# A graph network of four layers: the update pass reordered, the degree taken into the root, and eight row buffers in the heads pass

## The reference

```
x = layernorm(x + L0(x))   # two GAT convolutions, then concat(x, out2) @ Wu + bu
x = layernorm(x + L1(x))   # 12 heads of 64: relu(res + attention-weighted sum)
x = layernorm(x + L2(x))   # GCN: D^-1/2 A D^-1/2 (x W) + b
x = layernorm(x + L3(x))   # two GCN convolutions with a relu between
layernorm(x) = (x - mean) / sqrt(var + 1e-5)
```

## Time and profile before

| | us |
|---|---|
| median of 3 runs (lowest, highest) | 3884.01 (3877.66, 3886.38) |
| the profiled execution | 3883.69 |
| its span | 3881.9 |
| TensorE busy | 3556.3 (92%) |
| VectorE busy | 2481.6 (64%) |
| ScalarE busy | 1366.8 (35%) |
| GpSimd busy | 1092.4 (28%) |

### The profile page before, as it was taken

One profiled execution on the slowest core, in us unless ns is written; L12 is line 12 of the kernel. 1 busy time (PEld: TensorE's weight loads), 2 busy tenths in 40 slices (PEclk: granted clock), 3 DMA queues, 4 the chain that ended last, 5 costly groups with the idle time before them and its releaser, 6 DMA issues. The chain is left out here.

```text
span 3881.9 us, 64638 instructions
## 1 busy us (share of the span) xinstructions
PE 3556.3 (92%) x21125; PEld 3356.1 (86%) x21125; DVE 2481.6 (64%) x4955; ACT 1366.8 (35%) x1888; POOL 1092.4 (28%) x1533
## 2 busy tenths in 40 slices
PE   7999999999999888258996999998899998899999
PEld 6999999999999544138995999997899998799999
DVE  4877986158433588347996777776344443577777
ACT  2222232222222344115664344443333332344443
POOL 5540200414512100427774222221222221322221
PEclk9999999999999999679998999999999999999999
DMA  4777887658754688425665333334333333455554
GB/s 113 238 235 212 238 250 242 190 184 268 225 180 142 198 251 253 139 75 173 212 212 177 104 127 126 126 127 144 108 126 125 127 128 117 157 183 186 184 184 142
DMA packets 363376, 672.37 MB, mean 173 GB/s; under 512 B 100181, under 2 KB 193010, under 8 KB 363242
## 3 DMA queue, kind: packets, MB, share of 16 engines
q1 hardware_dynamic: 248154, 441.01, 37.3%
q10 hardware_dynamic: 70160, 155.79, 10.3%
q0 software_dynamic: 44928, 73.84, 6.8%
HBM read 429.79 MB, written 346.94 MB: 200 GB/s over the span
## 5 line engine op out<-in xcount | busy, mean ns | idle before, releaser
L716 DVE TENSOR_TENSOR fr_lo<-fr_turned_ps,fr_hi 128x768 fp32r<-128x768 f32 x158 | 150.4, 952 | 240.0 <-ACT fr_hi L1140 240.0
L1592 PE MATMUL up_prod<-w_up,up_ot 128*128 128x396 f32 x632 | 231.4, 510 | 40.9 <-DVE up_y L1496 40.9
L2408 DVE SCALAR_TENSOR_TENSOR c3a_y<-c3a_prod,dinv,next_const 128x768 f32<-128x768 f32 x79 | 80.4, 1018 | 288.8 <-PE c3a_prod L2564 288.8
L1284 PE MATMUL fr_prod<-fr_w_hi,fr_hi 128*128 128x396 f32 x948 | 257.1, 352 | 0.0
L1284 PE MATMUL fr_prod<-fr_wu_hi,fr_hi 128*128 128x396 f32 x948 | 254.7, 349 | 0.0
L1284 PE MATMUL fr_prod<-fr_w_lo,fr_hi 128*128 128x396 f32 x948 | 249.3, 344 | 0.0
L2564 PE MATMUL cv_prod<-next_w_hi,cv_hi 128*128 128x384 f32 x948 | 248.9, 344 | 0.0
L2564 PE MATMUL c3a_prod<-next_w_hi,c3a_hi 128*128 128x384 f32 x948 | 248.9, 344 | 0.0
L1284 PE MATMUL fr_prod<-fr_w_hi,fr_lo 128*128 128x396 f32 x948 | 248.7, 343 | 0.0
L2564 PE MATMUL c3b_prod<-next_w_hi,c3b_hi 128*128 128x384 f32 x948 | 248.6, 344 | 0.0
L1284 PE MATMUL fr_prod<-fr_wu_lo,fr_hi 128*128 128x396 f32 x948 | 248.3, 343 | 0.0
(11 more groups left out here) (588 smaller groups left out, 9109.0 us busy)
## 6 DMA issues: line engine op xcount, KB each, us to landing
fr_ins<-in_x_dram SPq DMA_DIRECT2D x156, 384.0 KB, 4.2
x<-fr_zrow SPq DMA_DIRECT2D x156, 384.0 KB
x<-up_x_o ACTq DMA_DIRECT2D x78, 396.5 KB, 3.5
h<-fr_outs SPq DMA_DIRECT2D x78, 396.0 KB
u<-fr_outs SPq DMA_DIRECT2D x78, 396.0 KB
up_ut<-u SPq DMA_DIRECT2D x78, 396.0 KB
agg<-fr_zrow SPq DMA_DIRECT2D x78, 390.0 KB
hds_row<-x SPq DMA_DIRECT2D x78, 384.0 KB, 3.2
```

The costliest lines, as they stand in the source:

```text
L716: v.tensor_tensor(lo[:, s2, :, :], turned_ps[:, 0:KC, :], hi[:, s2, :, :].bitcast(F32), ALU.subtract).then_inc(split_done, 1)
L1284: made = nc.tensor.matmul(prods[s2][:, bank, 0:c1 - c0], l[:, s2, s, :], w[:, s, c0:c1], start=(s == 0 and i == 0), stop=(s == KC - 1 and ...
L1592: made = nc.tensor.matmul(prods[s2][:, half, 0:HALFC], ot[:, s2, k, :], g["w_up"][:, k, half * HALFC:(half + 1) * HALFC], start=(k == 0), ...
L2408: v.scalar_tensor_tensor(y3, p3, g["dinv"][:, bass.ds(t, 1)], c3, ALU.mult, ALU.add).then_inc(prod_read, 1)
```

## The change

Update pass: y gets four buffers instead of two. VectorE's step does y and the statistics of tile t-2 first, and then the shift of tile t-3. The wait for the polish moves from before y to before the reciprocal, and asks for the tile before.

Heads pass and first convolution: 1 / sqrt(var + eps) times dinv is computed as 1 / sqrt(deg x var + deg x eps). The degree and its product with eps stand in two new columns, made in the first stage; ScalarE's root takes them as scale and bias, and VectorE's product with dinv goes.

Heads pass: eight buffers for the rows of x1, and the loop body of all engines there holds eight tiles; the other buffers stay four.

```
+            link(v.tensor_copy(g["deg"][:, :], pt["deg"][:, :]))
+            link(v.tensor_scalar(g["deg_eps"][:, :], pt["deg"][:, :], EPS, None, ALU.mult))
...
# update_pass
-        y = sb("y", [P, 2, CU])
+        y = sb("y", [P, UNROLL, CU])
...
                 dve.wait_ge(multiplied, t + 1)
-                if at_least(t, 2):
-                    dve.wait_ge(polished, t - 1)
-                v.tensor_tensor(y[:, s2, :].rearrange("p (a f) -> p a f", a=2), prods[s2][:, :, 0:HALFC],
+                v.tensor_tensor(y[:, slot, :].rearrange("p (a f) -> p a f", a=2), prods[s2][:, :, 0:HALFC],
...
             def shift_of(t, slot, turn):
                 s2 = slot % 2
                 dve.wait_ge(rooted, t + 1)
+                if at_least(t, 1):
+                    dve.wait_ge(polished, t)
                 v.reciprocal(rstd[:, s2, :], root[:, s2, :]).then_inc(shifted, 1)
...
             def step(t, slot, turn):
+                b = back(t, slot, turn, 2)
+                if at_least(t, 2) and live(b[0]):
+                    end(*b)
                 b = back(t, slot, turn, 3)
                 if at_least(t, 3) and live(b[0]):
                     shift_of(*b)
-                b = back(t, slot, turn, 2)
-                if at_least(t, 2) and live(b[0]):
-                    end(*b)
...
# heads_pass
-    H, F = 12, D
+    H, F, WIDE = 12, D, 2 * UNROLL
...
-        row, more = sb("row", [P, UNROLL, D]), sb("more", [P, UNROLL, AGG_W])
+        row, more = sb("row", [P, WIDE, D]), sb("more", [P, UNROLL, AGG_W])
...
-                if at_least(t, UNROLL):
-                    sp.wait_ge(prod_read, t - UNROLL + 1)
+                if at_least(t, WIDE):
+                    sp.wait_ge(prod_read, t - WIDE + 1)
                 sp.dma_start(row[0:rows_of(t), slot, :], tile_rows(x1, t)[:, 0:D]).then_inc(loaded[slot], 16)
-            over_tiles(sp, step)
+            over_tiles(sp, step, 0, WIDE)
...
                 v.reciprocal(rstd[:, s2, :], root[:, s2, :]).then_inc(shifted, 1)
-                dve.wait_ge(shifted, t * 3 + 1)
-                v.tensor_scalar(rstd[:, s2, :], rstd[:, s2, :], g["dinv"][:, bass.ds(t, 1)], None, ALU.mult).then_inc(shifted, 1)
-                dve.wait_ge(shifted, t * 3 + 2)
+                dve.wait_ge(shifted, t * 2 + 1)
...
-                nc.scalar.activation(root[:, slot % 2, :], mv[:, slot % 2, 1:2], ACT.Sqrt, bias=g["eps"][:, 0:1]).then_inc(rooted, 1)
+                nc.scalar.activation(root[:, slot % 2, :], mv[:, slot % 2, 1:2], ACT.Sqrt, bias=g["deg_eps"][:, bass.ds(t, 1)],
+                                     scale=g["deg"][:, bass.ds(t, 1)]).then_inc(rooted, 1)
```

More of the change, by code:

```diff
@@ L87, in at_least, with over_tiles, back @@
     return not isinstance(t, int) or t >= k
-def over_tiles(eng, step, drain=0):
-    for t in range(UNROLL):
+def over_tiles(eng, step, drain=0, unroll=UNROLL):
+    for t in range(unroll):
         step(t, t, 0)
[L95 to L104, removed]
+    with eng.Fori(1, NT // unroll) as i:
+        for j in range(unroll):
+            step(i * unroll + j, j, i)
+    for t in range(NT // unroll * unroll, NT + drain):
+        step(t, t % unroll, t // unroll)
+def back(t, slot, turn, lag, unroll=UNROLL):
+    return t - lag, (slot - lag) % unroll, turn + (slot - lag) // unroll
 def live(t):
@@ L1547, in polish @@
                     act.wait_ge(stored[slot], turn * 32)
-                nc.scalar.activation(x_o[:, slot, 0:D], y[:, s2, 0:D], ACT.Identity, bias=shift[:, s2, :],
+                nc.scalar.activation(x_o[:, slot, 0:D], y[:, slot, 0:D], ACT.Identity, bias=shift[:, s2, :],
                                      scale=rstd[:, s2, :]).then_inc(polished, 1)
@@ L2051, in heads_pass @@
         prods = [ctx.enter_context(nc.psum_tensor(f"hds_prod{i}", [P, 2, 512], F32)) for i in range(2)]
-        loaded = [sem(f"loaded{j}") for j in range(UNROLL)]
+        loaded = [sem(f"loaded{j}") for j in range(WIDE)]
         more_in = [sem(f"more_in{j}") for j in range(UNROLL)]
@@ L2102, in step @@
             def step(t, slot, turn):
-                b = back(t, slot, turn, -2)
+                b = back(t, slot, turn, -2, WIDE)
                 if live(b[0]):
                     fetch(*b)
-                b = back(t, slot, turn, -1)
+                b = back(t, slot, turn, -1, WIDE)
                 if live(b[0]):
@@ L2111, in _ @@
             scale(0, 0, 0)
-            over_tiles(pool, step)
+            over_tiles(pool, step, 0, WIDE)
         @block.vector
@@ L2167, in _ @@
             own(0, 0, 0)
-            over_tiles(dve, step, 3)
+            over_tiles(dve, step, 3, WIDE)
         @block.scalar
@@ L2238, in step @@
                     turn_over(t, slot, turn)
-                b = back(t, slot, turn, 1)
+                b = back(t, slot, turn, 1, WIDE)
                 if at_least(t, 1) and live(b[0]):
                     multiply(*b)
-            over_tiles(pe, step, 1)
+            over_tiles(pe, step, 1, WIDE)
 def conv_layer(nc, g, tag, table, out, weights, bias, res=None, first=False, last=False):
@@ L2256, in conv_layer @@
         L = 2 if apart else 1
-        K = 2 if last else 3
         rows_in = sb("row", [P, UNROLL, D])
@@ L2423, in shift_of @@
                 v.reciprocal(rstd[:, s2, :], root[:, s2, :]).then_inc(shifted, 1)
-                if not last:
-                    dve.wait_ge(shifted, t * K + 1)
-                    v.tensor_scalar(rstd[:, s2, :], rstd[:, s2, :], g["dinv"][:, bass.ds(t, 1)], None, ALU.mult).then_inc(shifted, 1)
-                dve.wait_ge(shifted, t * K + (K - 1))
+                dve.wait_ge(shifted, t * 2 + 1)
                 v.scalar_tensor_tensor(shift[:, s2, :], mv[:, s2, 0:1], -1.0, rstd[:, s2, :], ALU.mult, ALU.mult).then_inc(shifted, 1)
@@ L2478, in root_of @@
                 act.wait_ge(spread, t + 1)
-                nc.scalar.activation(root[:, slot % 2, :], mv[:, slot % 2, 1:2], ACT.Sqrt, bias=g["eps"][:, 0:1]).then_inc(rooted, 1)
+                if last:
+                    nc.scalar.activation(root[:, slot % 2, :], mv[:, slot % 2, 1:2], ACT.Sqrt, bias=g["eps"][:, 0:1]).then_inc(rooted, 1)
+                else:
+                    nc.scalar.activation(root[:, slot % 2, :], mv[:, slot % 2, 1:2], ACT.Sqrt, bias=g["deg_eps"][:, bass.ds(t, 1)],
+                                         scale=g["deg"][:, bass.ds(t, 1)]).then_inc(rooted, 1)
             def polish(t, slot, turn):
```

44 lines of the change are left out of this document (22 added, 22 removed).

## The result

| | before | after |
|---|---|---|
| median of 4 runs, us | 3881.35 (3877.66 to 3886.38) | 3821.43 (3819.79 to 3824.29) |
| profiled execution, us (span) | 3883.69 (3881.9) | 3824.29 (3822.6) |
| update pass, first to last y | 286.8, 3.677 a tile | 233.3, 2.991 a tile |
| heads pass, first to last y | 323.7, 4.150 a tile | 311.4, 3.992 a tile |
| the three convolutions, first to last y | 537.5, 537.6, 537.6 | 537.6, 537.6, 537.5 |

The ratio is 0.9846 (0.9829 to 0.9863): 60 us less, where I had forecast 3838 us, with 3826 as the best end of the range. In the spans the two passes give 53.5 + 12.3 = 65.8 us and the rest of the kernel takes 6.5 back.

What follows compares the result with a forecast made beforehand. Prediction: a VectorE wait chain bounds the update pass, TensorE nearly bounds the heads pass. 3883.7 less 35.6 (update) and 10.5 (heads) gave 3837.6, rounded to 3838 us; range 3826 to 3866 us.

Steps and rivals of the forecast that it cites:

- the DMA floor lies between 3.04 and 3.19 us: Update pass: least time a tile's 916 KB need, from 301 GB/s elsewhere and 287 GB/s at share 1.
- 3.22 us, a little above the highest: Update pass: tile period forecast just above the highest of three engine floors, saving 35.6 us.
- 3.64 - 0.36 - 0.20 = 3.08 us: Update pass: VectorE's period without the root and polish waits; 3.14 us on average with the loop turn's 3.31.
- Bounds: 3.12 us (43 us saved): Update pass: best case of the tile period; the worst was 3.5 us, 14 us saved.
- its floor is at most 3.12 us: Update pass: TensorE's time a tile, from its 0.52 us idle in each 3.64.
- hidden with about 1.1 us to spare: Update pass: the 1.01 us polish ends before VectorE's 2.3 us of y and statistics, so the moved wait costs nothing.
- TensorE's 3.99 us is the floor: Heads pass: TensorE limits each tile to 3.99 us, 311.2 us in all, 12.5 us below the pass then.
- The longer loop and the earlier rows: Heads pass: fewer loop turns bring VectorE's period to 3.68 us; earlier row loads end GpSimd's 25.6 us of waits.
- slack to catch up: Heads pass: VectorE gets 0.3 us of slack a tile and can catch up after a hold.
- Rival D: Heads pass: GpSimd's product, no longer paced by row loads, holds VectorE every tile; 4.98 us a tile, 3913 us; chance 0.06.
- A held VectorE slides into that gap: Heads pass: held VectorE moves into 2.3 us of y and statistics, where GpSimd's 1.5 us product disturbs nobody.
- By that rule the trace agrees, to 0.02 us: Heads pass: the shift's end matches GpSimd's product under the skill's rule that whichever came first excludes the other.

Runs made afterwards that it cites:

- update_only: The whole new update pass put in the kernel before, heads pass and first convolution as before: 3831.6 us, ratio 0.9884.
- four_rows_with_product: eight_rows_with_product with four row buffers in place of eight in the heads pass, loop of eight kept: 3823.55 us.
- eight_rows_with_product: Changed kernel with the product with dinv back on VectorE in the heads pass, eight row buffers and loop of eight kept: 3891.68 us, ratio 1.0029.
- late_shift: Changed kernel with a 128x256 memset on VectorE between reciprocal and shift in each tile of the heads pass: 3832.25 us.

## Why the prediction was right or wrong

**Update pass: mechanism right, size too small (35.6 forecast, 53.5 measured).** Three terms failed. First "the DMA floor lies between 3.04 and 3.19 us" and "3.22 us, a little above the highest": I had scaled the rate with the busy share (250/0.87 = 287 GB/s). The share is not proportional to the rate: 250 GB/s went with 0.87, 304 with 0.96, 351 with 1.045. The sentence from the Trainium skill (DMA: Bandwidth & Descriptors, Specifications; about 358 GB/s, no floor) was right, with 346 to 356 GB/s measured, and I set it aside for the rows; 301 GB/s at 0.92 should have told me that the scaling does not hold. This step costs 0.08 of the 0.23 us a tile between 3.22 and 2.99.

The other 0.15 is the second term, "3.64 - 0.36 - 0.20 = 3.08 us" and the mean of 3.14 from it. A turn of the loop takes 2.98 + 2.88 + 2.85 + 3.31 = 12.02 us, 3.005 a tile, and with the tiles written out at both ends 2.99: the turn was forecast right (3.31), the other three are 0.10 to 0.23 us shorter than 3.08, since the gaps shown as idle understate a wait. From aggregate to reciprocal 0.45 us went, not 0.36; from scores to y (1422.67 to 1422.87) 0.25, not 0.20 (0.45 us before, 1454.96 to 1455.41); and the reciprocal, 0.17 us long before, is recorded with 0.12. Where VectorE does not wait, the records of successive instructions overlap.

The third term is what put the result outside the range: the best case, "Bounds: 3.12 us (43 us saved)". It is the figure of "its floor is at most 3.12 us", 3.64 less TensorE's idle 0.52. An upper bound on TensorE's floor stood there as the least that a tile could take; TensorE's floor is about 2.88 and the pass reached 2.99, 53.5 us saved where the best case had 43. The step "hidden with about 1.1 us to spare" held: no wait before the reciprocal.

**Heads pass: the amount about right (10.5 forecast, 12.3 measured), the credit in part wrong.** TensorE's 3.99 us is the floor, as said, and taking the product away gives the gain, as said (311.8 us with four row buffers). The longer loop and the earlier rows, to which I gave a part, add nothing to it; with the product left in place they cost 55.3 us from first to last y, more than the update pass wins. Nor is it shown that slack to catch up counted: what went is the holds themselves. Their time above 0.16 us adds up to 10.3 of the 12.5 us lost in the kernel before (eight holds), 6.1 of 7.6 in update_only (four) and 4.1 of 4.4 in four_rows_with_product (three); in the changed kernel one hold is left. How much slack gives back after such a rare hold, these runs can't tell.

Rival D named 4.98 us a tile, measured 4.86 in eight_rows_with_product. The mechanism is D's, the closeness is luck: D's sum is 3.68 + 1.3 for a kernel without the product, while this run has it (3.87 + 0.47/8 = 3.93) and its holds cost 1.02 each (1.18 less 0.16). D gave its chance as a matter of GpSimd's pace. It missed that the product removed and the buffers added meet in the same 0.3 us. "A held VectorE slides into that gap" was wrong: `own` releases GpSimd's product, so a held VectorE takes GpSimd along.

"By that rule the trace agrees, to 0.02 us" was read too quickly. The end agrees, but the shift of the earlier trace rows is recorded from 0.70 us ahead of the product, so by "whichever came first" it should not have been held. The rule of the Trainium skill (SBUF — State Buffer, Who interferes with whom) agrees on the form of the instruction: with two tensors in SBUF the shift is held for 1.17 us, with one it takes 0.21. On who comes first it agrees with the recorded starts in most tiles and not in late_shift, nor in five holds named below.

**The rest: the convolutions as said** (within 0.1 us each). The 6.5 us given back are spread: 1.3 ahead of the update pass, where the two new operations of the first stage account for some 0.5 by the prediction's estimate, 1.2 between the two passes, 2.0 ahead of the first convolution and 1.8 between the convolutions. Over 17 traces all that lies outside the five passes differs between 1657 and 1673 us, so that a single profile proves nothing of it; the medians, 59.9 us apart against 65.8 in the passes, ask for some 6 us too. Whether a few us of it are real stays open.

## What to carry to other kernels

Test a suspected floor by adding a known load to each engine that looks full: of three that read 0.92 to 1.0, one was the bound, one 0.11 us below and one 13% below. Do not scale a DMA rate by its busy share, nor size a wait by its idle time alone, nor use an upper bound on one engine's floor as the best case of a range. Where GpSimd works in parallel with VectorE, count the instructions of VectorE with two SBUF tensors that follow the release of GpSimd's work, and put them ahead of it or write them with one tensor: a faster supply of GpSimd can turn rare holds into steady ones.

## What the runs showed of the hardware

A VectorE instruction on a single column (128x1) with two SBUF tensors was held for the rest of a GpSimd tensor_tensor, 1.17 to 1.29 us in the median; a tensor_scalar on the same data in the same place was not (0.21 us). The y step, which reads one tensor in PSUM and one in SBUF, ran beside the product unheld (0.94 to 0.96 us).

It goes the other way round too. GpSimd's small tensor_tensor ahead of each gather (L83) takes 0.19 us alone; started behind VectorE's add, which has two SBUF tensors, it lasted until 0.05 us behind the add's end, in 20 of 79 tiles of the kernel before:

```profile
1852.42 1.02 DVE L2128 SCALAR_TENSOR_TENSOR hds_x<-hds_more,has_in,hds_x 128x768 f32<-128x768 f32 x1 [0.40 <-POOL hds_x L2099]
1852.60 0.90 POOL L83 TENSOR_TENSOR hds_scrap_p<-ones 128x1 f32<-128x1 f32 x1
...
1853.64 1.07 POOL L2090 DMA_INDIRECT hds_more<-agg,hds_ix  x1
```

Five holds do not fit the reading above: they are recorded from 0.34 to 0.70 us ahead of the product that they end with, two in the kernel before (one is that of the earlier trace rows), two in update_only and one in four_rows_with_product. In all five GpSimd was in the gather's instruction (the last line shows it for the earlier trace rows) and the product followed within 0.03 us. But 25 other shifts of the kernel before fell in the same place and were not held, so these five stay unexplained.
